# A graph kernel's first pass: subtracting relu(bias) behind layer one on ScalarE, and all eight record loads begun by SyncE

## The reference

```python
# layer 0: edges grouped by src
seg_sum = segment_sum(edge_attr, row); cnt = segment_sum(1, row)
seg_max = where(cnt > 0, segment_max(edge_attr, row), 0)
seg_mean = seg_sum / maximum(cnt, 1)
h = relu(concat([seg_sum, seg_max, seg_mean, u]) @ W1 + b1)
x = x + h @ W2 + b2
# layer 1: rows gathered by src and summed by dst
h = maximum(layernorm(x), 0)
x = x + relu(segment_sum(h[src], dst) @ W.T + b)
```

## Time and profile before

| | |
|---|---|
| median of 3 runs | 1252.31 us (1250.37 to 1253.11) |
| profiled execution | 1251.71 us |
| its span on the core | 1249.8 us |
| outside the span | 1.9 us |
| steady part of the first pass | about 235 to 695 us of the span |
| fast path chosen, table stored | about 708 and 721 us |
| second pass | from about 721 us on |

### The profile page before, as it was taken

The page is one execution under the profiler, slowest core; times in us unless marked ns, Lnnn a source line. Parts: engine busy times, 40 slices in busy tenths (PEclk is TensorE's granted clock), DMA queues, the critical chain, the costliest instruction groups (busy, mean ns, idle before and its releaser), DMA issues.

```text
span 1249.8 us, 20773 instructions
## 1 busy us (share of the span) xinstructions
PE 968.8 (78%) x5818; PEld 765.5 (61%) x5818; DVE 1024.1 (82%) x2720; ACT 280.4 (22%) x681; POOL 784.5 (63%) x836
## 2 busy tenths in 40 slices
PE   0122017999999999999999814888988989788988
PEld 0011014777777777777777613776776777676777
DVE  8888896899999999999999635677767777777874
ACT  1451032222222222222222111111112112111210
POOL 3000047777777777777778367777777777777750
PEclk9996556899999999999999855889898888989889
DMA  1000012788999899898897544778787777787765
GB/s 65 0 0 0 0 41 69 176 223 221 241 239 236 223 244 234 233 232 218 234 238 204 161 145 105 181 200 224 187 233 201 206 198 208 206 211 220 201 172 164
DMA packets 317563, 218.51 MB, mean 175 GB/s; under 512 B 223428, under 2 KB 255140, under 8 KB 317444
## 3 DMA queue, kind: packets, MB, share of 16 engines
q1 hardware_dynamic: 182100, 135.41, 38.6%
q10 hardware_dynamic: 110256, 62.42, 19.0%
q0 software_dynamic: 25088, 19.32, 8.7%
HBM read 137.51 MB, written 79.45 MB: 174 GB/s over the span
## 4 chain that ended last, share of the span: by engine, by line
DVE 47%; PE 16%; DMA 12%; POOL 9%; issue 7%; ACTq 6%; ACT 3%; DVEq 0%; POOLq 0%; SPq 0%
POOL xa L555 9%; DMA xa<-node_table,gi 7%; DVE feats L1077 7%; DVE feats L1075 7%; DVE oneh L1098 5%; DMA win<-records 4%; DVE dout L1117 4%; ACTq L679 4%; PE p_m L1364 3%; DVE kb L923 2%; DVE rec L1125 2%; DVE ka L923 2%; DVE shared L1098 2%; PE p_u L1376 2%; PE p_t L1376 2%
## 5 line engine op out<-in xcount | busy, mean ns | idle before, releaser
L536 POOL DMA_INDIRECT xa<-in_edge_attr_dram,gi x392 | 373.0, 952 | 232.2 <-issue 115.6
L555 POOL DMA_INDIRECT xa<-node_table,gi x392 | 370.1, 944 | 142.3 <-issue 103.1
L689 ACT ACTIVATE hid<-p_z,bias_z 128x512 f32<-128x512 f32 x98 | 113.5, 1158 | 239.3 <-issue 226.5
L1077 DVE TENSOR_TENSOR_SCAN feats<-c_rows,feats,p_g 32x512 f32<-32x512 f32 x97 | 123.3, 1271 | 1.4
L1075 DVE TENSOR_TENSOR_SCAN feats<-c_rows,feats,p_g 64x512 f32<-64x512 f32 x97 | 122.5, 1263 | 0.0
L1405 PE MATMUL p_g<-ident,hn 128*128 128x128 f32 x196 | 46.6, 325 | 97.4 <-DVE hn L1179 97.2
L742 ACT ACTIVATE sd<-mv,eps_t 128x4 f32<-128x4 f32 x98 | 29.2, 298 | 407.0 <-DVE mv L1170 350.0
L1098 DVE SCALAR_TENSOR_TENSOR shared<-p_m,node_of 112x1024 f32<-112x1024 f32 x98 | 117.2, 1196 | 3.8 <-PE p_u L1376 1.4
L1364 PE MATMUL p_m<-w_s,hid 128*128 128x64 f32 x784 | 109.3, 283 | 14.0 <-ACT hid L689 13.4
L1098 DVE SCALAR_TENSOR_TENSOR oneh<-p_m,node_of 112x1024 f32<-112x1024 f32 x98 | 119.3, 1217 | 0.2
L1381 PE MATMUL p_u<-one 128*128 128x512 f32 x230 | 115.9, 590 | 0.1
(11 more groups left out here) (257 smaller groups left out, 1577.1 us busy)
## 6 DMA issues: line engine op xcount, KB each, us to landing
win<-records SPq DMA_DIRECT2D x980, 28.9 KB
records<-rec ACTq DMA_DIRECT2D x196, 132.0 KB
din<-in_x_dram SPq DMA_DIRECT2D x49, 512.0 KB
node_table<-dout SPq DMA_DIRECT2D x49, 512.0 KB, 4.3
din<-node_table SPq DMA_DIRECT2D x43, 512.0 KB, 4.8
out_dram<-dout SPq DMA_DIRECT2D x43, 512.0 KB
c_rows<-rows_src ACTq DMA_DIRECT2D x141, 128.0 KB
win<-records ACTq DMA_DIRECT2D x588, 28.9 KB
```

What stands on the lines that cost most here:

```text
L536: g.indirect_dma_start(out=xa[n % XRING][:, t, 0:FE], out_offset=None, in_=edge_attr, in_offset=bass.IndirectOffsetOnAxis(ap=gi[0][:, BT * ...
L555: g.indirect_dma_start(out=xa[k % XRING][:, t, :], out_offset=None, in_=T, in_offset=bass.IndirectOffsetOnAxis(ap=gi[1][:, BT * n + t:BT * ...
L689: s.activation(hid[n % 2][:, :].rearrange("p (t n) -> p n t", n=P), p_z[n % 2][:, :].rearrange("p (n t) -> p n t", t=BT), ACT.Relu, bias=b ...
L1077: v.tensor_tensor_scan(f[64:96, :], c[64:96, at:at + BLK], p_g[n % 2][0:32, :], first[64:96], ALU.min, ALU.max).then_inc(feats_ok, 1)
```

## The change

ACT now subtracts the constant ahead of layer two. `less_r0` = −relu(bias) is a column of 128 values; a second ACTIVATE (Identity with that bias) over the 128x512 tile follows `hidden`, waits for the first one, and only then is `hid_ok` counted up. Layer two thus gives the difference directly, and the sums need only be moved: ACT does that too, with a copy of 128x256 behind the copy of the keys, as it did in the second pass already. DVE's `less_constant` and `c_neg` are gone. SP begins all eight window loads of the first pass and loads eight starts; ACT's `upper_windows` is gone from the first pass. The second pass keeps its code.

```diff
-SP_LOADS = (6, 4)
+SP_LOADS = (8, 4)
...
             def hidden(n):
                 act.wait_ge(z_ok, n + 1)
                 s.activation(hid[n % 2][:, :].rearrange("p (t n) -> p n t", n=P), p_z[n % 2][:, :].rearrange("p (n t) -> p n t", t=BT),
-                             ACT.Relu, bias=bias_z[:, :]).then_inc(hid_ok, 1)
+                             ACT.Relu, bias=bias_z[:, :]).then_inc(hid_raw, 1)
+                act.wait_ge(hid_raw, n + 1)
+                s.activation(hid[n % 2][:, :], hid[n % 2][:, :], ACT.Identity, bias=less_r0[:, :]).then_inc(hid_ok, 1)
...
-                keys = s.copy(rec[k % RRING][:, :, KEY], rn[side][:, BT * n:BT * (n + 1)])
-                if side == 0:
-                    keys.then_inc(keyed, 1)
-                else:
-                    s.copy(rec[k % RRING][:, :, 0:D], delta(k)).then_inc(copied, 1)
+                s.copy(rec[k % RRING][:, :, KEY], rn[side][:, BT * n:BT * (n + 1)])
+                s.copy(rec[k % RRING][:, :, 0:D], delta(k)).then_inc(copied, 1)
...
-                if n == SRC_WIN:
-                    act.wait_ge(s_tail, 64)
-                    act.wait_ge(s_start, 1)
-                if valid(n - SRC_WIN):
-                    upper_windows(0, n - SRC_WIN)
...
+                v.tensor_scalar(less_r0[:, :], bias_z[:, :], 0.0, -1.0, ALU.max, ALU.mult)
...
-                v.tensor_scalar(c_neg[:, :], p_g[0][:, 0:D], -1.0, None, ALU.mult)
...
-            def less_constant(n):
-
-                dve.wait_ge(m_ok, n + 1)
-                v.tensor_tensor(rec[n % RRING][:, :, 0:D], delta(n), c_neg[:, :].unsqueeze(1).to_broadcast([P, BT, D]), ALU.add).then_inc(copied, 1)
...
-                if valid(n - SRC_REC):
-                    less_constant(n - SRC_REC)
```

More of the change, by code:

```diff
@@ L131, in build @@
         r0 = sb("r0", [P, P])
-        c_neg = sb("c_neg", [P, D])
+        less_r0 = sb("less_r0", [P, 1])
         added_rows = sb("added_rows", [P, D])
@@ L268, in build @@
         z_ok, hid_ok, m_ok = sem("z_ok"), sem("hid_ok"), sem("m_ok")
-        copied, keyed = sem("records_copied"), sem("keys_copied")
+        copied, hid_raw = sem("records_copied"), sem("hidden_not_yet_less")
         keys_up = sem("window_keys_in_psum")
@@ L694, in record @@
                 act.wait_ge(m_ok, k + 1)
-                keys = s.copy(rec[k % RRING][:, :, KEY], rn[side][:, BT * n:BT * (n + 1)])
-                if side == 0:
-                    keys.then_inc(keyed, 1)
-                else:
-                    s.copy(rec[k % RRING][:, :, 0:D], delta(k)).then_inc(copied, 1)
+                s.copy(rec[k % RRING][:, :, KEY], rn[side][:, BT * n:BT * (n + 1)])
+                s.copy(rec[k % RRING][:, :, 0:D], delta(k)).then_inc(copied, 1)
             def store_rec(side, n):
                 k = BLOCKS * side + n
-                if side == 0:
-                    act.wait_ge(keyed, k + 1)
                 act.wait_ge(copied, k + 1)
```

## The result

The changed kernel took 1264.18 us in the median of 4 runs (1263.69 to 1264.73), the kernel before 1252.7 on the same chips. The ratio is 1.0100, 95% interval 1.0085 to 1.0116: 1% slower, where 1246 us and a small gain were forecast. The profiled execution took 1264.58 us with a span of 1262.8, 13.0 more than before. The second pass kept its length: from POOL's first gather of table rows to the end of the span are 1262.8 − 735.2 = 527.6 us, before 1249.8 − 721.6 = 528.2. All of the loss lies in the first pass. Of all executions in this document only one, the profiled one of e1 (1324.6 us), was in a slow state of the chip: e1's ratio and median leave it out, and its trace is read for the order of the work, not for exact times.

The account below looks back on a forecast made before the run. SP's instruction stream was to become last in each step (5.01 us), ahead of PE (4.84) and DVE (4.5). Last keys 1.8 us earlier plus 4.3 off the tail gave 6.1 us less, 1246 us, range 1235 to 1280.

Parts of the forecast that it names:

- SP's step: SP's instruction stream in the first pass: 4.36 us of work plus two DMAs and a changed register load, 5.01 us.
- the 4.3 us taken off behind the last keys: End of first pass: with block 96 expanded long before, keys to last addition take 4.2 us instead of 8.5.
- 0.47 us for each added DMA: SP in the first pass: two more DMAs a step at 0.47 us each, 0.94 in all.
- Rough SP steps: Rival, SP in the first pass: long loads and issues count once SP is last; step 5.16 us, 1259 us; chance 0.17.
- first rival: Rival: eight values load as cheaply as four (0.30 us), SP's step 4.81, POOL caps the gain; 1237 us; chance 0.18.
- The register load of eight values: SP in the first pass: eight starts loaded as two fours in 0.50 us, bounds 0.30 and 0.94.
- ACT's own path would be free: ACT in the first pass: the difference is ready 0.7 us before the old relu ended, so the added Identity costs nothing.
- the cap by POOL's count: End of first pass: POOL's count can't be done before 694.9 us, so the last keys come at 698.0 at the earliest.
- growing load: Rival, SP in the first pass: register load grows with the count to 0.94 us, step 5.45; 1285 us; chance 0.18.

Follow-up runs that it names:

- e1: Changed kernel's ACT part alone: ACT subtracts and moves the sums, but SP begins six window loads and ACT two, as before; 1.0465 of the kernel before, 1307.6 us.
- e3: Changed kernel with the first pass's dense-row loads begun by ACT instead of SP; 1.0137 of the kernel before, 1268.1 us.
- e4: Changed kernel with fewer bytes in the dense-row and c_rows loads from the third pair on, same number of DMAs; 1.0034 of the kernel before, 1253.8 us.
- e6: Changed kernel with both edits, dense loads begun by ACT and fewer bytes in dense rows and c_rows; 0.9965 of the kernel before, 1244.9 us.
- e5: The changed kernel itself run again as yardstick; 1.0120 of the kernel before, 1263.3 us.
- e12: Changed kernel with the choice of path in step 103 instead of 101; 1.0103 of the kernel before, 1262.8 us.
- e7: Changed kernel, but ACT begins two of the eight window loads again, behind the relu instead of ahead of it; 0.9975 of the kernel before, 1246.2 us.
- e10: Changed kernel with a second register load of the same eight starts in each first-pass step; one execution, 1349.1 us.
- e13: The kernel of e7 with the choice of path in step 103; 0.9891 of the kernel before, 1236.7 us.

## Why the prediction was wrong

The place was right: SP's stream became the last thing in each step, PE and DVE had time to spare, ACT's second ACTIVATE was covered. Two terms of the sum failed: SP's step, forecast at 5.01 us where 5.08 decided and measured at 5.18, and the 4.3 us taken off behind the last keys. The first has a wrong idea in it and not only a wrong size: it took the length of an issue as fixed, and e3 shows that it was not.

**The issues on SP.** The prediction took 0.47 us for each added DMA, from a group's length divided by its count. That left out the gap behind a group; from the start of one issue to the start of the next are 0.480 us in the mean in the kernel before and 0.519 in the changed one. Worked out over the changed kernel, an issue costs 0.417, its register move 0.029 and the gaps 0.067, so 0.513: two are 1.03 in place of 0.94. And the prediction let the six old issues stay as they were. They became dearer by 0.026 each, 0.16 a step. The register load worked the other way. The prediction took the old load off with its median, 0.79, from a step that is a mean; the mean of the old load is 0.887. From there to 0.534, the mean of the new one, are 0.35 less, not 0.29, so this slip, and not only the good guess for eight values, brought the sum nearer. 0.09 + 0.16 − 0.06 = 0.19 turns 5.01 into 5.20; measured are 5.21 between 300 and 600 us and 5.18 from window to window over the pass (466.3 us for 90 steps from 250.01 to 716.29). 90 × 0.17 = 15.4 us. "Rough SP steps" was the rival that happened, for 1259, and it had 0.17. Its argument against itself, that 4.36 is already a mean, did not hold, because that mean belonged to an SP that waited an eighth of its time (38.9 of 300.5 us). e3, e4 and e6 show that the length of an issue went with the bytes in flight and with what ACT begins at the same time.

**The tail.** The prediction let block 96 be expanded long before the last keys and took off 4.3 us. In the kernel's order PE stands before that block until the choice is made, and DVE makes it behind the one-hot matrix of 96. So in the first profile 0.9 us came on instead: 5.2 in all. The prediction used the order of the choice on DVE for its first rival without reading the same step on PE. Order and clock share these 5.2 us. In e5 the order was the same and the clock came back to 2.4 GHz for the last block: 6.1 us passed, 1.9 more than the forecast's 4.2. The other 3.3 came with the lower clock of the first profile, where the last filler and expansion took 2.02 + 3.51 us for 1.08 + 1.89, and block 96's expansion 3.52 for 2.81. So the order failed in every profile of this kernel, and the size 5.2 holds for the first one. Where PE has block 96 behind it, as the prediction assumed, the expansion ends 3.65 us behind the keys (e12).

The rest is small: the last keys were read 1.4 us behind the last issue, not 2.9 (−1.5), and the window from which the 90 steps are counted began 0.45 us later (at 250.01). −6.1 + 15.4 + 5.2 − 1.5 + 0.5 = 13.5; the table came 13.6 us later in the profile (POOL's first gather at 735.2 for 721.6). In e5 it came at 732.2, 3.0 earlier, nearly all of it from the end.

**What was right.** The register load of eight values (0.53 for 0.50; its bounds were 0.30 and 0.94); that ACT's own path would be free, as PE never waited for it (e1 shows what it costs with the loads ahead of it: 58 us); the cap by POOL's count (e7). The rival "growing load" did not happen. The Trainium skill's floor of 600 ns for a `tensor_load` (DMA: Bandwidth & Descriptors, Latency and other measured facts) was not seen: eight values took 0.53. The Trainium skill's sentence that beginning DMAs on several engines only saves the sequencer's time (the same page, Issuing engines are not separate DMA queues) describes e7 against e5: the same DMAs, and 17 us saved. For one DMA that time is small, 0.42 us to begin a load whose landing took 4.19; nine of them a step, with a register load, fill SP's whole step.

**What stays open.** What makes an issue long. Fewer bytes make long issues rarer (30 to 10, 48 to 21), the dense load on ACT makes them more frequent (30 to 48, 10 to 21), a slower step makes them rarer (13 of 384 in e10), and splitting the windows over two queues makes them rarer at more GB/s (13 of 360 in e7, though 20 of 354 in e13). A backlog in the queue that SP fills, or two engines that begin DMAs at the same time, would both fit part of this; no run separates them. So it is shown that the loss comes with SP's stream, but not how much of SP's time is its own work and how much is such a wait. Also open is why every second one of the second register loads in e10 takes 1.38 us.

## What to carry to other kernels

Before moving DMA issues to a queue, add up that queue's whole step, with gaps, register loads and the mean of an issue, and compare it with the step of the loop: an engine that is never busy in the profile can be the one that is last. Take means, not medians, when one term is exchanged in a step that is itself a mean. An issue's length measured while the queue had time to spare was too low for a queue without any: 7% too low in the changed kernel, 13% in e3. If an issue is in the way of an instruction, try first to put it behind that instruction on the same engine; here this was worth 1.3% over moving it to the other queue.

## What the runs showed of the hardware

- A TENSOR_LOAD from SBUF took 0.28 us for one value and 0.30 for four, 0.53 for eight, at least 0.71 for six and at least 0.91 for seven; on ACT 0.50 for two, at least 0.71 for three and 0.32 for four. Loading eight and using six was cheaper than loading six (e7: 0.53 for 0.79 in the median).
- With all eight loads on one queue the DMA engines were busy for 0.95 to 0.98 of the time at 224 GB/s, with six and two for 0.91 at 235 GB/s. The higher busy share went with fewer bytes moved.
- PE's clock was at either of its levels at the end of the pass in two profiles of the same kernel, and the last addition came 3.3 us sooner behind the last keys where it was back at 2.4 GHz for the last block.
- Taking an instruction of 0.25 us a step from an SP that never waits gave nothing (e3), as its other issues and register loads grew by 0.24.
